# A masked-attention kernel: the mask in three transfers of its own, behind the first block's keys

## The reference

```
q = target_key @ W_target.T
k = einsum('bld,ed->ble', item_keys, W_item)
v = einsum('bld,ed->ble', item_values, W_value)
scores = einsum('bd,bld->bl', q, k) / 8
scores = scores + -1e8 * (1.0 - mask)
w = softmax(scores, axis=1)
return einsum('bl,bld->bd', w, v)        # B, L, D = 512, 200, 64
```

## Time and profile before

| | |
|---|---|
| median of 3 runs | 133.96 us (133.62 to 134.03) |
| profiled execution | 133.99 us, of which the span of instructions is 132.2 us |
| TensorE matmuls busy | 72.5 us, 55% of the span |
| VectorE, ScalarE, GpSimd busy | 19.6, 7.8 and 5.3 us |
| read from memory | 53.07 MB, a mean of 402 GB/s over the span |
| mean granted TensorE clock | 0.815 of full speed |

### The profile page before, as it was taken

The page is one execution under the profiler, slowest core; times in us unless marked ns, Lnnn a source line. Parts: engine busy times, 40 slices in busy tenths (PEclk is TensorE's granted clock), DMA queues, the critical chain, the costliest instruction groups (busy, mean ns, idle before and its releaser), DMA issues.

```text
span 132.2 us, 1303 instructions
## 1 busy us (share of the span) xinstructions
PE 72.5 (55%) x536; PEld 22.7 (17%) x536; DVE 19.6 (15%) x55; ACT 7.8 (6%) x26; POOL 5.3 (4%) x18
## 2 busy tenths in 40 slices
PE   0000007992499214992089522993069839949981
PEld 0000003331122011221012111231011122302250
DVE  6000002004200500005100310004200130033060
ACT  3000001003000000003000010002000000011000
POOL 7400000000000000001000000001000000001000
PEclk9999999998569955599559995589658975797698
DMA  8699799799979997999899889979998989999900
GB/s 272 272 544 510 306 520 434 310 496 496 434 310 485 496 434 326 482 498 389 373 480 496 372 387 481 498 327 420 398 472 387 480 387 455 403 443 406 393 18 10
DMA packets 2450, 53.22 MB, mean 402 GB/s; under 512 B 784, under 2 KB 784, under 8 KB 1040
## 3 DMA queue, kind: packets, MB, share of 16 engines
q1 hardware_dynamic: 1872, 53.07, 93.5%
q10 hardware_dynamic: 576, 0.13, 0.5%
HBM read 53.07 MB, written 0.13 MB: 402 GB/s over the span
## 4 chain that ended last, share of the span: by engine, by line
DMA 57%; PE 25%; issue 12%; DVE 3%; ACT 1%; POOLq 0%; SPq 0%; DVEq 0%; ACTq 0%
DMA value<-values 57%; PE ps_context L457 7%; PE ps_scores L438 6%; PE ps_context L466 4%; PE ps_context L460 3%; PE ps_context L474 3%; PE ps_small L485 1%; DVE context L381 1%; DVE context_slots L377 1%; ACT expd L263 0%; DVE biased L341 0%; DVE second_biased L338 0%; DVE neg_max L344 0%; SPq L185 0%; POOLq L74 0%
## 5 line engine op out<-in xcount | busy, mean ns | idle before, releaser
L438 PE MATMUL ps_scores<-first_tile,sta_query 128*32 128x400 f32 x256 | 30.9, 651 | 9.0 <-DMA first_tile<-keys 8.4
L457 PE MATMUL ps_context<-value,sta_full 128*32 128x512 f32 x64 | 13.5, 989 | 10.8 <-DMA value<-values 10.8
L438 PEld LDWEIGHTS ps_scores<-first_tile,sta_query 128*32 128x32 f32 x256 | 9.6, 138 | 28.5 <-issue 19.6
L417 PE MATMUL ps_small<-first_tile 64*64 64x128 f32 x4 | 0.7, 444 | 19.9 <-DMA first_tile<-first 19.9
L377 DVE TENSOR_TENSOR context_slots<-ps_context,in_octet 128x512 f32<-128x512 f32 x4 | 2.8, 692 | 38.0 <-PE ps_context L474 32.5
L338 DVE SCALAR_TENSOR_TENSOR second_biased<-ps_scores,in_pair,mask_bias 128x200 f32<-128x200 f32 x4 | 1.7, 426 | 43.6 <-PE ps_scores L438 43.6
L466 PE MATMUL ps_context<-value,sta_half 128*32 128x512 f32 x64 | 7.7, 598 | 0.0
L239 POOL COPY half_twice<-expd 128x128 f32<-128x128 f32 x4 | 1.4, 345 | 113.2 <-ACT expd L263 113.2
L444 PE MATMUL ps_turn_full<-ident,expd 128*128 128x128 f32 x4 | 1.3, 328 | 8.2 <-ACT expd L263 8.2
L474 PE MATMUL ps_context<-value,sta_full 128*32 128x512 f32 x48 | 5.7, 592 | 0.0
L460 PE MATMUL ps_context<-value,sta_eighth 128*128 128x512 f32 x8 | 5.5, 775 | 0.0
(11 more groups left out here) (48 smaller groups left out, 34.5 us busy)
## 6 DMA issues: line engine op xcount, KB each, us to landing
value<-values SPq DMA_DIRECT2D x3, 6400.0 KB, 23.0
first_tile<-keys SPq DMA_DIRECT2D x2, 6400.0 KB, 22.0
first_tile<-first SPq DMA_DIRECT2D x1, 7024.0 KB, 19.0
first_tile<-keys SPq DMA_DIRECT2D x2, 3200.0 KB, 18.2
value<-values SPq DMA_DIRECT2D x1, 2304.0 KB, 12.4
value<-values SPq DMA_DIRECT2D x1, 2048.0 KB, 16.8
value<-values SPq DMA_DIRECT2D x1, 1280.0 KB, 19.4
value<-values SPq DMA_DIRECT2D x1, 512.0 KB, 20.2
```

The source lines that it names most:

```text
L438: last = nc.tensor.matmul(ps_scores[g * GU:(g + 1) * GU, 0:QB], window(sta_query, g, k), key[:, c:c + QB], start=k == 0, stop=k == QUADS - 1)
L457: nc.tensor.matmul(ps_context[g * GU:(g + 1) * GU, :], window(sta_full, g, k), value[:, c:c + OB], start=k == 0, stop=False)
```

## The change

The mask is no longer packed into the rows of the first transfer; it has a tensor (`mask_rows`, 128 rows of 3,200 bytes), a tile (`mask`) and a semaphore (`s_mask`) of its own. It is loaded by three transfers, of rows 0 to 87, 88 to 119 and 120 to 127, issued from SyncE behind the first transfer and ahead of the first values. VectorE waits for all three before it makes the bias. The total of bytes is unchanged; the rows of the first transfer are 52,992 bytes long instead of 56,192.

```diff
-def masked_attention_kernel(nc, first, keys, values, out):
+def masked_attention_kernel(nc, first, mask_rows, keys, values, out):
...
-    MASK = W_VALUE + D
-    FIRST = MASK + NBLK * L
+    FIRST = W_VALUE + D
+
+    MASK_ENDS = (88, 120, P)
...
-        mask = first_tile[:, MASK:FIRST].bitcast(mybir.dt.int32)
+        mask = sb("mask", [P, NBLK * L], mybir.dt.int32)
...
                 if n == 0:
                     sp.dma_start(first_tile[:], first).then_inc(s_key, 16)
+                    begin = 0
+                    for end in MASK_ENDS:
+                        sp.dma_start(mask[begin:end, :], mask_rows[begin:end, :]).then_inc(s_mask, 16)
+                        begin = end
...
-            dve.wait_ge(s_key, 16)
-            nc.vector.tensor_scalar(mask_bias[:].rearrange("p n l -> p (n l)"), mask, -1.0, MASKED, ALU.add, ALU.mult).then_inc(s_mask_bias, 1)
+            dve.wait_ge(s_mask, 16 * len(MASK_ENDS))
+            nc.vector.tensor_scalar(mask_bias[:].rearrange("p n l -> p (n l)"), mask[:], -1.0, MASKED, ALU.add,
+                                    ALU.mult).then_inc(s_mask_bias, 1)
```

More of the change, by code:

```diff
@@ L88, in masked_attention_kernel @@
         targets = first_tile[:, TARGETS:W_VALUE]
-        w_value_twice = first_tile[:, W_VALUE:MASK]
-        mask = first_tile[:, MASK:FIRST].bitcast(mybir.dt.int32)
+        w_value_twice = first_tile[:, W_VALUE:FIRST]
+        mask = sb("mask", [P, NBLK * L], mybir.dt.int32)
         value = sb("value", [P, V_COLS])
@@ L155, in masked_attention_kernel @@
         s_sta_query = sem("s_sta_query")
+        s_mask = sem("s_mask")
         s_mask_bias = sem("s_mask_bias")
@@ L551 @@
     mask_rows = np.ascontiguousarray(mask.reshape(NBLK, P, L).transpose(1, 0, 2).reshape(P, NBLK * L))
-    small = np.concatenate([small, mask_rows.view(np.float32)], axis=1)
     arrays = {
         "first": np.concatenate([k[0], small], axis=1),
+        "mask_rows": mask_rows,
         "keys": k[1:],
```

## The result

The changed kernel takes 136.24 us (median of 6 runs, 136.1 to 136.99), the kernel before 133.67 us beside it (6 runs, 133.42 to 134.03): a ratio of 1.02, interval 1.0177 to 1.0222. The profiled execution took 136.99 us, the longest of its six; its span is 135.3 us. So the difference of the two profiles, 3.0 us, is 0.4 more than that of the medians.

The account below looks back on a forecast made before the run. The DMA stream bounds the kernel up to the third values' landing at 96.9, on which the end hangs. The terms sum to 133.99 - 0.72 + 0 = 133.27, forecast as 133.3 us, range 132.9 to 134.4.

Parts of the forecast that it names:

- Moved: Mask rows per engine go from 8 to 11, 10 or 2, at 0.12 us a row: +0.36, +0.24, -0.72 us.
- case A: The forecast: the late engine is among five light ones, so landings from 51 us come 0.72 earlier; 133.3 us, chance 0.55.
- The late engine: One DMA engine falls 1.2 to 1.3 us behind between 35 and 51 us and sets all later landings.
- B: Rival: the late engine gets more mask rows; heavy gives 134.35 us, one of three middle engines 134.2; chance 0.2.
- a service fetch goes to an engine at the end of the row: Judgement that q8's instruction fetch, 0.75 us, falls on a last engine rather than one picked evenly.
- Small-transfer cost: zero: Three more queued mask transfers cost no visible fixed time; taken as zero, bounded at 0.1 us.
- Wait on VectorE: The mask's scaling waits for the mask, landing by 20.3, before its start at about 21.6: nothing waits.
- issues on SyncE: Three issues ahead of the values take 1.4 us, free because the engines are busy until 19.
- split into 11, 16 and 8: Mask transfers of 88, 32 and 8 rows go to 11, 16 and 8 engines, as equal whole rows.
- First start at 18.9: PE's first start moves from 19.90 to about 18.9, as the first transfer loses 410 KB, 0.96 us; worth nothing.
- Rival D: PE's clock rises at the same instants, so half speed takes the gain; 0.18 us left, 133.8 us, chance 0.13.
- P: Theory from the experiments, not the prediction: rows cut out of place make engines share a way into SBUF and slow down.

Follow-up runs that it names:

- e1: The changed kernel with the mask in one transfer of 128 rows instead of 88, 32 and 8: 134.13 us, ratio 1.002 to the kernel before.
- e6: As e4 with three of the extra transfers instead of one, to partitions 0, 1 and 2 and every fourth behind them: 136.23 us.
- e9: As e6, but each of the three extra transfers has 11 rows instead of 8, loading three engines more: 138.41 us.
- e2: The changed kernel with its three mask transfers cut by columns (550, 200, 50), all 128 rows in each: 134.20 us.
- e8: As e1, with 128 bytes of zeros added to each row of the first transfer: 133.97 us.
- e3: The changed kernel with the mask in two transfers of 96 and 32 rows, even engine loads: 135.30 us.
- e7: The changed kernel with the mask in two transfers of 64 and 64 rows, even engine loads: 136.19 us.
- e10: The changed kernel with the mask in two transfers of 120 and 8 rows, one engine light: 136.53 us.
- e5: As e4, but the extra transfer's eight rows go to partitions 120 to 127: 137.40 us.
- e4: As e1, plus one extra transfer of 8 rows of 19.2 KB to partitions 0, 4, ... 28 of an unused tile: 134.76 us.

## Why the prediction was wrong

- **The step that failed** is the term under "Moved": "At 0.12 us a row: +0.36, +0.24 and -0.72 us." It priced a row by its engine alone. The 0.12 came from transfers in which every engine writes to its own partitions, and holds there (127 ns per row on the mean in e1). In the cut transfers the same row costs 0.215 on the mean, and it slows the transfers ahead and behind. The real term is about +2.1 us (e1 to the change). Against e1 the packets of an engine grow on the mean by 0.70 us for its mask rows, 1.00 for its first value row and 0.12 for the rows of the first transfer; the larger part falls on a neighbour, for which the prediction had no term, and 0.3 of the 2.1 us stand in none of these three kinds of packet.
- With it falls **case A**. A light engine gains nothing: what its partitions must take is unchanged, and other engines now send it. The five engines that begin the values first, presumably those with two mask rows, take 3.2 to 3.6 us for that row and end it at 22.2 to 22.9; in e1 all sixteen have ended it by 22.1.
- **The late engine** was rightly found to be one engine that loses its time between 35 and 51 us and keeps the lag, and it is not light: e6 and e9 put it among the three middle ones. By load alone (B's middle case, +0.24) the time would have been 133.9 (over the kernel before) or 134.4 (over e1). B had the sign by a mechanism that is a tenth of the loss. The judgement that a service fetch goes to an engine at the end of the row was wrong for this one. That the packet of q8 is behind the lag fits the traces, at 1.4 us with the row behind it instead of the 0.75 of the prediction.
- **"Small-transfer cost: zero"** held for the number of transfers: e2, with three and 200-byte rows, is e1. The Trainium skill's advice against splitting ("DMA: Bandwidth & Descriptors", section "Rules for kernel authors") gives as its reason that transfers to parts of the partitions serialize, since they use the same engines. The advice was right here, 2.1 us for the cut, and I set it aside too soon, having weighed only the fixed cost. The rows of before held only transfers of all 128 rows, so they could refute the price per transfer and not the rest.
- **Wait on VectorE, issues on SyncE, split into 11, 16 and 8**: right, as the rows above show. **First start at 18.9**: wrong by 2.2 us. In e1 it is at 19.65, so 1.5 of them are the cut mask's traffic reaching back into the transfer ahead of it, and 0.7 belong to what stays open below.
- **The range** (132.9 to 134.4) took the bounds of a row's price from the scatter of the existing transfers, 10%. No row bounded the price of a row *out of its place*, and the text knew that no such transfer was in the trace. The upper end should have allowed for two engines on one path, 0.96 us more for half speed alone.
- **Rival D**, the clock, played no part in the total: the third values' landing is 3.12 us later and the late matmuls start 3.01 later (129.30 for 126.29).

What stays open: the 0.3 to 0.5 us between before and e1, e2 or e8, which all have the mask in whole transfers of its own. It is at the edge of what the runs tell (three intervals from 0.9998, 1.0002 and 1.0003 up). In e1's profile, the longest of its ten, the third values land at 97.93 against 96.94. Part of it is seen in the first transfer: in the kernel before the engines end their last rows of it within 0.5 us (19.06 to 19.54), in e1 within 1.3 (17.95 to 19.25), so the last one is only 0.3 earlier where the bytes say 0.96. The row length is not it (e8). Also open is why the even cuts differ so much (96 and 32 costs 1.2 over e1, 64 and 64 costs 2.1).

No version tried is faster than the kernel before, which has the mask packed into the first transfer.

## What to carry to other kernels

In these runs a load of all 128 partitions had each DMA engine on its own partitions (mask rows of 127 ns in e1). A load of fewer rows deals them out over as many engines as divide their number (the packet counts), by P in the order of their place in the transfer, and engines then meet on the same partitions' path and slow each other and both neighbours in the queue (1.2 to 2.4 us in e3, e7, e10 and the change). Split a small tensor by columns, or not at all, and not by rows to even out engines. When a forecast rests on an operation of a shape that the trace doesn't hold, its price has to be bounded from the worst neighbour that is conceivable, not from the scatter of the ones that are there.

## What the hardware showed that I had not expected

- The same 154 KB from the same eight engines cost 2.64 us more when sent to eight adjacent partitions instead of every fourth one (e5 against e4), and a transfer queued ahead of it landed 2.6 us later.
- 410 KB of mask, 0.8% of the traffic, delays a stream of 53 MB by 2% when its rows are out of place.
- One engine falls behind by 1.1 to 1.6 us between the first values and the second keys, in every kernel here whose extra load does not hide it, and 45 us of streaming up to the third values do not make it up. It goes with one 16 KB packet of a service queue (0.94 to 1.07 us) and the slow row behind it (2.39 us instead of 1.89).
